# Layer 1's routed rows added to the residual in memory instead of stored and merged later

## The reference

```python
x = x + tanh(g_xattn[0]) * wkv(w, u, k=layernorm(x), v=ctx)
x = x + tanh(g_ffn[0])   * ffn0(layernorm(x))   # 8 experts of 256, top 2, plus a shared expert
x = x + tanh(g_xattn[1]) * attention(layernorm(x), ctx, ctx)   # 16 heads, causal
x = x + tanh(g_ffn[1])   * ffn1(layernorm(x))   # 64 experts of 352, top 6, plus a shared expert
```

```python
ew, ei = top_k(scores, 2); ew = softmax(ew)
routed = sum over the two chosen e of ew[e] * (silu(xf @ w_gate[e].T) * (xf @ w_up[e].T)) @ w_down[e].T
```

## Time and profile before

| | |
|---|---|
| median of 3 runs | 2472.98 us (2466.5 to 2476.64) |
| the profiled execution's own time | 2463.79 us |
| its span | 2462.1 us |
| TensorE's mean granted clock | 0.928 of full speed |
| busy share of the span: PE, DVE, POOL, ACT | 84%, 50%, 33%, 30% |
| phase 3, from its first load to the first load of phase 4 | 572.35 to 1006.33 us |
| stores to `y0` in phase 3 | 72, from 613.3 to 999.6 us |
| merges in phase 4 | 32, 2.36 us each |

### The profile page before, as it was taken

How to read it: one execution, slowest core, us unless ns; L and a number is a source line. 1 busy time by engine, 2 the same in 40 slices (tenths; PEclk the granted TensorE clock), 3 DMA queues, 4 the chain that set the end, 5 groups by cost and what they waited for, 6 DMA issues and landing times. The chain is left out here.

```text
span 2462.1 us, 38884 instructions
## 1 busy us (share of the span) xinstructions
PE 2079.0 (84%) x11938; PEld 1408.1 (57%) x11939; DVE 1242.4 (50%) x2853; ACT 737.1 (30%) x2144; POOL 817.9 (33%) x822
## 2 busy tenths in 40 slices
PE   1899888894999999479999999999999846878786
PEld 1666666662555555257777777777777622333332
DVE  5777888863222222246676766666675501211221
ACT  2222222212222222244444444444444100111110
POOL 4455555531333333212333333433332401111211
PEclk9999999997999999659999999999999868888888
DMA  8232222213332232321111112211110089999994
GB/s 267 78 86 85 85 71 83 85 43 103 96 94 90 93 94 91 129 81 61 61 61 62 61 66 100 79 62 61 62 61 18 18 311 358 345 343 352 368 352 105
DMA packets 134409, 315.28 MB, mean 128 GB/s; under 512 B 37811, under 2 KB 46003, under 8 KB 126069
## 3 DMA queue, kind: packets, MB, share of 16 engines
q1 hardware_dynamic: 107380, 260.68, 30.5%
q0 software_dynamic: 26880, 52.68, 7.8%
HBM read 253.13 MB, written 62.33 MB: 128 GB/s over the span
## 5 line engine op out<-in xcount | busy, mean ns | idle before, releaser
L1422 ACT ACTIVATE attn_pr<-attn_score_ps,attn_nmax 128x128 f32<-128x128 f32 (+1 forms) x512 | 208.4, 419 | 194.7 <-DVE attn_nmax L1550 194.7
L948 PE MATMUL routed_gu_ps<-first_ffn_wgu,routed_xT 128*128 x576 | 261.2, 596 | 0.0
L1513 POOL DMA_INDIRECT list<-attn_pair,attn_pos x192 | 191.6, 998 | 74.4 <-issue 74.1
L310 PE MATMUL attn_ffn_ps<-attn_xnT_high,attn_wgu_high 128*128 128x256 f32 x704 | 210.1, 298 | 4.1 <-DVE attn_hT_low L1641 3.3
L310 PE MATMUL attn_ffn_ps<-attn_xnT_high,attn_wgu_low 128*128 128x256 f32 x704 | 201.5, 286 | 3.1 <-issue 3.1
L310 PE MATMUL attn_ffn_ps<-attn_xnT_low,attn_wgu_high 128*128 128x256 f32 x704 | 201.5, 286 | 1.4 <-issue 1.4
L1880 PE MATMUL routed_y_ps<-routed_wdn_a,routed_hT 128*64 128x512 f32 (+1 forms) x192 | 118.3, 766 | 81.8 <-DVE routed_hT L1953 81.8
L282 POOL TENSOR_SCALAR attn_norm_var_eps<-attn_norm_mean_var 128x2 f32<-128x2 f32 x32 | 7.9, 248 | 536.8 <-DVE attn_norm_mean_var L276 536.8
L948 PEld LDWEIGHTS routed_gu_ps<-first_ffn_wgu,routed_xT 128*128 128x128 f32 x576 | 104.9, 192 | 104.6 <-issue 104.6
L1550 DVE TENSOR_REDUCE attn_nmax<-attn_score_ps 128x2 f32<-128x256 f32 (+1 forms) x256 | 130.4, 551 | 63.0 <-PE attn_score_ps L1279 59.0
L1968 DVE TENSOR_SCALAR routed_same<-routed_ids_ps,routed_token 128x128 f32<-128x128 f32 x32 | 11.2, 351 | 297.4 <-DMA out<-routed_ym,routed_place 295.0
(11 more groups left out here) (254 smaller groups left out, 5031.9 us busy)
## 6 DMA issues: line engine op xcount, KB each, us to landing
routed_wgu_a<-in_w_gu SPq DMA_DIRECT2D x32, 1408.0 KB
routed_wgu_b<-in_w_gu SPq DMA_DIRECT2D x32, 1408.0 KB
wkv_x<-in_x SPq DMA_DIRECT2D x32, 512.0 KB, 3.6
attn_y<-y SPq DMA_DIRECT2D x32, 512.0 KB
routed_wdn_a<-in_w_down SPq DMA_DIRECT2D x32, 512.0 KB
routed_wdn_b<-in_w_down SPq DMA_DIRECT2D x32, 512.0 KB
wkv_vT<-in_ctxT SPq DMA_DIRECT2D x16, 512.0 KB
xn<-wkv_xn SPq DMA_DIRECT2D x16, 512.0 KB
```

Of the source, the lines that this page charges most:

```text
L310: ins = nc.tensor.matmul(out, a[i], b[j], start=start and n == 0, stop=stop and n == 2)
L948: ins = nc.tensor.matmul(gu_ps[t.s % 2][:], xT[t.s % 2][:, k, :], wgu[:, bass.ds(e, 1), k, :].rearrange("p a n -> p (a n)"), start=(k == 0 ...
L1422: nc.scalar.activation(pr[u % 2][:, a, j:2 * j + 1, :].rearrange("p k t -> p (k t)"), score_ps[:, a, j * P:(2 * j + 1) * P], ACT.Exp, bias ...
L1513: nc.gpsimd.indirect_dma_start(io["list1"], bass.IndirectOffsetOnAxis(ap=pos[b.s][:, j, k:k + 1], axis=0), pair[b.s][:, j, k, :], None, bo ...
```

## The change

Phase 3 no longer stores its rows to `y0`. Each tile's rows are added to `x2` in memory by an accumulating indirect transfer, at the row number that the gather already uses. Two tiles may hold the same token (its two choices), so each of these transfers first waits until the one before has landed. `y0`, its loads and the POOL merges of phase 4 are gone, the list entries have two words in place of three, and `x2` gets 128 spare rows (zeroed in `setup`) for the unused slots; these rows are now transferred too, where the store skipped them.

```diff
@@ setup: one more spare block zeroed, one memset fewer
-                for d in (io["xn0"], io["xn1"], io["out"]):
+                for d in (io["xn0"], io["xn1"], io["x2"], io["out"]):
                     sp.dma_start(d[N:N + DUMMY, :], zeros[:]).then_inc(stored, 16)
-                nc.vector.memset(fill[:, :, 1], UNUSED).then_inc(dve_s, 1)
@@ wkv_phase, slots: two small operations a turn fewer
-                    posts.did(v.tensor_copy(pair[b.s][:, :, :, 0], c.token_no[:].unsqueeze(2).to_broadcast([P, TJ, K0])))
-                    for k in range(K0):
-                        numbered = posts.did(v.tensor_scalar(pair[b.s][:, :, k, 1], c.token_no[:], float(k * N), None, ALU.add))
+                    numbered = posts.did(v.tensor_copy(pair[b.s][:, :, :, 0], c.token_no[:].unsqueeze(2).to_broadcast([P, TJ, K0])))
@@ routed0_phase, place
                     pool.wait_ge(ys_s, t.i + 1)
                     alone(pool)
-                    nc.gpsimd.indirect_dma_start(io["y0"], bass.IndirectOffsetOnAxis(ap=pair[t.s][:, 1:2].bitcast(U32), axis=0),
-                                                 ys[t.s % SLOTS0][:], None, bounds_check=K0 * N - 1, oob_is_err=False).then_inc(placed[t.s % SLOTS0], 16)
+                    if not t.first:
+                        pool.wait_ge(placed[t.before().s % SLOTS0], 16 * uses(t.before()))
+                        alone(pool)
+                    nc.gpsimd.indirect_dma_start(io["x2"], bass.IndirectOffsetOnAxis(ap=pair[t.s][:, 0:1].bitcast(U32), axis=0),
+                                                 ys[t.s % SLOTS0][:], None, compute_op=ALU.add).then_inc(placed[t.s % SLOTS0], 16)
@@ attention_phase, load (SP)
                     sp.dma_start(x[b.s][:], rows(io["x2"], b)).then_inc(x_in[b.s], 16)
-                    wait(sp, merged, K0 * b.i)
-                    alone(sp)
-                    for k in range(K0):
-                        sp.dma_start(y0[:, k], io["y0"][bass.ds(b.i * T + k * N, T), :].rearrange("(j p) c -> p j c", p=P)
-                                     ).then_inc(x_in[b.s], 16)
@@ attention_phase, turn (POOL)
-                        if u in (1, 2) and not b.last:
-                            merge(b.after(), (u - 1,))
@@ attention_phase, norm_pre (DVE)
-                    dve.wait_ge(merged, K0 * (b.i + 1))
+                    dve.wait_ge(x_in[b.s], 16 * (b.round + 1))
```

More of the change, by code:

```diff
@@ L24 @@
 TILES0 = N * K0 // P + E0
-UNUSED = 2 * K0 * N
 LIST0 = E0 * N + P
@@ L35 @@
 WAYS0, SLOTS0, AHEAD0 = 8, 4, 3
-POST_STEPS0, TABLE_STEPS0 = 24, 15
+POST_STEPS0, TABLE_STEPS0 = 22, 15
 UNITS = HEADS // 2
@@ L168, in setup @@
         slot_low = m.sb("slot_low", [P, LIST0 // P], I32)
-        fill = m.sb("fill", [P, LIST0 // P, 3], I32)
+        fill = m.sb("fill", [P, LIST0 // P, 2], I32)
         fill1 = m.sb("fill1", [P, E1 * CAP // P, 2], I32)
@@ L181, in _ @@
                 sp.wait_ge(made, 3)
-                for d in (io["xn0"], io["xn1"], io["out"]):
+                for d in (io["xn0"], io["xn1"], io["x2"], io["out"]):
                     sp.dma_start(d[N:N + DUMMY, :], zeros[:]).then_inc(stored, 16)
-                sp.wait_ge(dve_s, 7)
+                sp.wait_ge(dve_s, 6)
                 sp.dma_start(io["list0"].rearrange("(p j) c -> p (j c)", p=P),
@@ L189, in _ @@
                 sp.wait_ge(const_s, 64)
-                sp.wait_ge(stored, 5 * 16)
+                sp.wait_ge(stored, 6 * 16)
             @block.gpsimd
@@ L207, in _ @@
                                allow_small_or_imprecise_dtypes=True).then_inc(made, 1)
-                nc.gpsimd.memset(fill[:, :, 2], 0).then_inc(made, 1)
+                nc.gpsimd.memset(fill[:, :, 1], 0).then_inc(made, 1)
                 nc.gpsimd.memset(fill1[:], 0).then_inc(made, 1)
@@ L346, in wkv_phase @@
         pos = [m.sb(f"pos_{s}", [P, TJ, K0], U32) for s in range(2)]
-        pair = [m.sb(f"pair_{s}", [P, TJ, K0, 3], I32) for s in range(2)]
+        pair = [m.sb(f"pair_{s}", [P, TJ, K0, 2], I32) for s in range(2)]
         gap = m.sb("gap", [P, TJ, 2])
@@ L741, in slots @@
                         c.base0[:].unsqueeze(1).to_broadcast([P, TJ, E0]), ALU.add))
-                    posts.did(v.tensor_copy(pair[b.s][:, :, :, 0], c.token_no[:].unsqueeze(2).to_broadcast([P, TJ, K0])))
-                    for k in range(K0):
-                        numbered = posts.did(v.tensor_scalar(pair[b.s][:, :, k, 1], c.token_no[:], float(k * N), None, ALU.add))
+                    numbered = posts.did(v.tensor_copy(pair[b.s][:, :, :, 0], c.token_no[:].unsqueeze(2).to_broadcast([P, TJ, K0])))
                     dve.wait_ge(tgap_s, b.i + 1)
                     for k, sign in enumerate((c.gate_half, c.gate_neg)):
-                        posts.did(v.scalar_tensor_tensor(pair[b.s][:, :, k, 2].bitcast(F32), tgap[:, :, 0], sign[:, 2:3],
+                        posts.did(v.scalar_tensor_tensor(pair[b.s][:, :, k, 1].bitcast(F32), tgap[:, :, 0], sign[:, 2:3],
                                                          c.gate_half[:, 2:3].to_broadcast([P, TJ]), ALU.mult, ALU.add))
@@ L854, in routed0_phase @@
         expert_i, row_i = m.sb("expert_i", [P, TILES0], I32), m.sb("row_i", [P, TILES0], I32)
-        pair = [m.sb(f"pair_{s}", [P, 3], I32) for s in range(WAYS0)]
+        pair = [m.sb(f"pair_{s}", [P, 2], I32) for s in range(WAYS0)]
         xg = [m.sb(f"xg_{s}", [P, C]) for s in range(SLOTS0)]
@@ L1062, in scaled @@
                     wait(dve, placed[t.s % SLOTS0], 16 * (uses(t) - 1))
-                    v.tensor_scalar(ys[t.s % SLOTS0][:], y_ps[t.s % 2][:], pair[t.s][:, 2:3].bitcast(F32), None, ALU.mult).then_inc(ys_s, 1)
+                    v.tensor_scalar(ys[t.s % SLOTS0][:], y_ps[t.s % 2][:], pair[t.s][:, 1:2].bitcast(F32), None, ALU.mult).then_inc(ys_s, 1)
                 def turn(t):
@@ L1086, in attention_phase @@
         ctx = [m.sb(f"ctx_{s}", [P, TJ, C]) for s in range(2)]
-        y0 = m.sb("y0", [P, K0, TJ, C])
         q_tok = m.sb("q_tok", [P, TJ, C])
@@ L1495, in _ @@
             def _(pool):
-                def merge(b, some=range(K0)):
-                    for k in some:
-                        if k:
-                            pool.wait_ge(merged, K0 * b.i + k)
-                        else:
-                            pool.wait_ge(x_in[b.s], 16 * (1 + K0) * (b.round + 1))
-                        nc.gpsimd.tensor_tensor(x[b.s][:], x[b.s][:], y0[:, k], ALU.add).then_inc(merged, 1)
                 def scatter(b, u):
@@ L1526, in turn @@
                             scatter(b.before().before(), u)
-                merge(FIRST)
                 norm1.pool(nc, pool, FIRST)
@@ L2066, in laid_out @@
     }
-SCRATCH = {"x2": ((N, C), F32), "xn0": ((N + DUMMY, C), F32), "xn1": ((N + DUMMY, C), F32),
-           "list0": ((LIST0, 3), I32), "y0": ((K0 * N, C), F32), "list1": ((E1 * CAP, 2), I32)}
+SCRATCH = {"x2": ((N + DUMMY, C), F32), "xn0": ((N + DUMMY, C), F32), "xn1": ((N + DUMMY, C), F32),
+           "list0": ((LIST0, 2), I32), "list1": ((E1 * CAP, 2), I32)}
 def kernel(**inputs):
```

1 line of the change is left out of this document (removed).

## The result

The changed kernel takes 2497.7 us, median of four runs (2494.8 to 2498.5), against 2471.3 for the kernel before on the same chip: a ratio of 1.0128, 95% interval 1.0100 to 1.0156. It is slower. The profiled execution took 2497.3 us with a span of 2495.6, which is 33.5 us over before's 2462.1. The time lies inside the range of the prediction, but the likeliest case there was "no change"; slower had 0.35.

What follows compares the result with a forecast made beforehand. PE was taken to set the pace in phases 2, 3 and 4. The terms 14.8 + 1.7 - 8.8 - 1.2 gave +6.5 us: 2470.3 for the profiled execution, about 2479 as median, range 2462 to 2517.

Steps and rivals of the forecast that it cites:

- the likeliest case: Whole kernel: a phase 3 step of 5.48 to 5.73 us, sum -6 to +12 us, central +6.5; chance 0.45.
- Term 1: Phase 3's serial chain of 72 adding transfers: 5.65 us a step against 5.44, +14.8 us over 71 steps.
- Term 2: Tail of phase 3: the barrier waits for the last add's landing, 4.7 us against about 3.4; +1.7 us.
- Term 3: Start of phase 4: DVE's statistics wait for one load, 3.87 us in place of 12.7; -8.8 us.
- Term 5: Phase 2 and setup: two small DVE operations a turn go, a third of their time counted; -1.2 us.
- Term 4: Rest of phase 4: 30 more merges leave POOL, but they lie in its idle time; 0 us.
- Rival C: Phase 4 turns: merges delay DVE or the next layernorm by 1 us a turn, so removal gains 15 us; chance 0.05.
- rival A: Phase 3: the adding chain becomes the bound, slower by over 0.5% from a 5.74 us step on; chance 0.34.

Runs made afterwards that it cites:

- e3: Kernel before, with each phase 3 store to `y0` waiting for the landing of the store before it; ratio 0.9997 to the kernel before.
- e4: Kernel before, its phase 3 stores made adding transfers to `y0` rows zeroed in setup, none waiting for another; ratio 1.0169, median 2470.6 us without the zeroing.
- e8: Changed kernel with two useless POOL adds of the merges' size put back into each phase 4 turn; ratio 1.0008 to the kernel before.
- e2: Phases 1 to 3 of the kernel before with phase 4 of the changed kernel, layer 1's routed rows left out; ratio 1.0017 to the kernel before.
- e5: Changed kernel with SP's store of normalised rows (xn1) put ahead of the output store in phase 4; ratio 1.0103 to the kernel before.
- e9: Changed kernel with all twelve list scatters of a phase 4 turn moved behind the next sequence's first norm; ratio 1.0599 to the kernel before.
- e10: Changed kernel with each pair of phase 4 list scatters waiting for the landing of the pair before, no work added; ratio 0.9995 to the kernel before.
- e6: Kernel before with SP's xn1 store held until the last matmul ahead of its logits has ended; ratio 0.9981 to the kernel before.

## Why the prediction came out as it did

**Term 1, +14.8: right in kind, small in size.** The step is 5.70 us, not 5.65; 71 steps give +18.7. Landing is 4.9 us where I took 4.70 and 0.10 for the gather behind it; the restart is the rest, 0.80 (0.85 taken). e3 and e4 show that it takes the landing of an add and the wait together.

**Term 2, +1.7: too small.** 10.98 us in place of 6.70 is +4.3. I compared two landings, 4.7 and 3.4, and allowed 0.4 for skipped rows. But the last tile holds unused slots alone. Its store of before moves nothing (0.00 MB from 999.6 us on), and that of the changed kernel moves 0.26 MB, its 128 spare rows. The last transfer of the changed kernel, then that of e4, which adds but skips (us to landing):

```profile
x<-routed_ys,routed_pair POOLq DMA_INDIRECT x1, 5.0
...
y<-routed_ys,routed_pair POOLq DMA_INDIRECT x1, 2.7
```

e4's tail is 8.7 us (1043.3 to 1051.99), the changed kernel's 10.98: the 2.3 us between them are what the spare rows take to land. The 2.0 from 6.70 to 8.7 come with the adding transfers and were not taken apart. The two-chain kernels have the long tail too (1001.4 to 1012.4).

**Term 3, -8.8: right.** 3.84 us from load to statistics; 3.87 was forecast.

**Term 5, -1.2:** -0.7 (phase 3's first load of a list entry at 578.27 us, before 578.95).

**Term 4, "phase 4 otherwise: 0": the step that failed.** The other four terms measure 18.7 + 4.3 - 8.8 - 0.7 = +13.5 of the 33.5 us. The other 20 are the longer turns: 682.0 - 663.1 = 18.9 us over 12 of them, and about 1 us net in the first turns, the last and phase 5. By the medians, 26.3 us apart, some 13 are left for this term in place of 20. I wrote that the merges lie in POOL's idle time and so cost nothing to remove. That held for POOL's time: with pads in their place the 12 intervals are 656.4 us, 6.7 under before. But POOL's wait for DVE said nothing of what stands behind the merges in POOL's own queue: they kept eight scatters from going out in one row, and in a row these hold up DVE and leave gaps in PE, whose clock then falls. Rival C looked at the same place with the opposite sign. The pads bear it out in part, at 0.6 us a turn once the scatters are spaced, where it had 1; no rival had a turn that gets longer. That the time fell inside the range is luck: the part of it above 2485 stood for rival A, whose condition, a step above 5.74 us, did not occur.

With e8's pads the ratio is 1.0008, 2 us over before with an interval from -4 to +8; the likeliest case had +6.5 for a phase 4 without a new wait. That agrees, but two errors offset each other in it: turns that are 6.7 us shorter in sum, and Terms 1 and 2 that are 6.5 us larger than forecast.

**Shown and not shown.** Shown: the stands named "remote" appear with eight or twelve scatters in a row (changed, e2, e5, e9, and the kernel before in its last turns), in the changed kernel mostly end 2.4 us after the start of the eighth, and go when the row is broken, by work (e8) or by waits (e10). PE's gaps at its first routing matmuls come and go with them (27 in the changed kernel, 26 in e2, 23 in e5; none in e8 and e10). Argued, from PE's busy time in one execution of each: that the falls of the clock follow these gaps. They also come without a row of eight, in one turn of e3, one of e6 and two of e4. Not shown: through what the scatters hold up DVE and PE. Their own packets, 222 in the 10 us of the eight shown, take 1.9% of the DMA engines' time, so it is not their bandwidth; two 512 KB stores run beside them (DMA share 0.47 in that stretch), but the same stores run in e8 and e10 without a stand. Late instructions are a candidate. In the turn shown, a 16 KB packet of an instruction queue (q8) began 2.5 us after the first routing matmul (1222.2 against 1219.71), in before 2.0 us (1211.7 against 1209.79). But in five of the eleven turns with gaps the packet had landed by 0.7 us after the first of these matmuls, and PE's first gap still came at 3.2 us; in e8 there are no gaps wherever it lands. The Trainium skill (Runtime: NRT & Kernel Launch, "Instruction fetch mechanics") says that each sequencer fetches blocks by a DMA queue of its own and that this is mostly hidden; nothing here shows such a fetch for DVE inside a stand before the maxima, and it stays open.

## What to carry to other kernels

An instruction in an engine's idle time can still do something: it spaces what stands behind it in that engine's queue, so before it is removed, read which DMA issues close up. Look for a wait of another engine, with no releaser named, beside a burst of small indirect transfers, and pace such bursts by their own landings, which cost nothing here and gained 0.46% even in the kernel before. Before a skip of unused rows is given up, ask whether the last transfer of a phase is one of them: here its landing took 5.0 us in place of 2.7. A chain of transfers that must land one after the other is free up to the pace of the bottleneck engine and costs each tenth of a microsecond beyond it times its length; two chains into two arrays bring it back under.

## What was not expected of the hardware

Scatters of 128 entries each, issued every 1.27 us, stopped VectorE for 4.5 us after eight and 8.9 us after twelve, while they themselves used under 3% of the DMA engines. Gaps of 2.0 to 3.3 us after every second one removed this. Beside such a stand PE had gaps of its own, without a wait for VectorE: it was busy for 0.65 of 1.5 us and was then granted half its clock for some 3 us, and by PE's busy time that is most of why such a turn is 2 to 3 us longer.
